# Routed tiles: the gated rows' transpose leads each round, the products come one round later

## The chip, the cores and the metric

The kernel runs on one core of one Trainium2 chip. The metric is the device time of one execution in microseconds, lower is better; of several executions the median counts. Engines are named as in the profile: PE is TensorE (PEld its weight loads), ACT is ScalarE, DVE is VectorE, POOL is GpSimd, SP is the engine that issues most DMAs.

## The reference

Two batches of 1024 tokens of 256 numbers pass through four sublayers: differential attention, a gated feed-forward with a Walsh-Hadamard transform, attention with 16 heads, and a mixture of experts. Each is added to its input and normalized. The change lies in the routed half of the last one:

```python
h12 = jnp.einsum('td,ehd->teh', flat_x, w12)      # 8 experts, 2 x 128 columns each
h1, h2 = jnp.split(h12, 2, axis=-1)
h = jax.nn.silu(h1) * h2
out_e = jnp.einsum('teh,edh->ted', h, w3)
routed_out = jnp.einsum('ted,te->td', out_e, combine).reshape(b, s, d)
```

`combine` is zero but for the two experts that a token has picked.

## The kernel before, in words

The kernel is one program with an instruction stream for each engine, written out by hand; semaphores order the engines against each other, and within an engine the order is that of the code. It does the two batches one after the other.

For the routed half the kernel computes a token only for its two experts. Each pair of a token and an expert gets a row in a list sorted by expert, GpSimd scatters the tokens to it in memory (`xs`), and SP loads the list back into `xg` as 23 tiles (`TILES`) of 128 rows, each tile with one expert (`owner(k)`, read from a register: a register step or two, the REGISTER_ALU rows, and an ISA row that sets the address stand ahead of the product). Then `routed(b)` takes each tile k through these steps:

- TensorE transposes the tile's 256 columns in two pieces (`turn_tokens`, L1033) into PSUM (`xt_bank[k % 2]`).
- The products are made in three passes of a high and a low part (`pass3`, L408 to L410). So ScalarE copies the transposed tile to `xr_h` (L1499), and VectorE subtracts that from it and has `xr_l` (L1916).
- TensorE multiplies with the expert's gate and up weights (`gate_up_tile`: six products, shown as `ps<-E_h,xr_h` and the like, into `xt_bank[2 + k % 2]`).
- ScalarE makes the SiLU (`silu_r`, L1511), VectorE the gated rows `Hr` (L1932).
- TensorE transposes these (`turn_gated`, L1055) into the one bank `ring[0]`. ScalarE copies them to `hr_h` (L1505), VectorE makes `hr_l` (L1925).
- TensorE multiplies with the expert's last weights (`down_tile`: three products, `ps<-E_h,hr_h`, into the one bank `ring[1]`), ScalarE copies the result into `xg` (L1515), and GpSimd stores it to its rows in `ys` (L2347).

The steps of different tiles overlap. Round i of the loop holds, on TensorE, the token transposes of tile i, the gated transpose of tile i - 3, the products of tile i - 1 and the result of tile i - 4. ScalarE's round has xr_h of i, hr_h of i - 3, the SiLU of i - 1 and the result copy of i - 4; VectorE's has xr_l of i, hr_l of i - 3 and Hr of i - 1. Buffers are used in turn by two (`k % 2`). What matters among the waits: the gated transpose waits for the hr_l of the tile before (`rh_lo`), as they share the bank, and for its own Hr (`rm_done`); the product of a tile waits for its xr_l (`rx_lo`); the token transposes wait for the xr_l of two tiles back and for the load of `xg` (`xg_in`); a result's product waits for its hr_l and for the copy of the result before (`ry_copy`).

In the first rounds there is other work too. TensorE makes the last two results of the shared half (`down`) in rounds 0 and 1, VectorE takes these into `X` (`take`, L1632, four instructions, 1.4 us in all), and in rounds 2, 4 and 10 it works out store addresses in three small operations (`destinations`, L1903 to L1908). In the first batch both takes fall into the routed stage, at rounds 1 and 2; in the second batch the stage begins four steps before the end of the shared half, and the second take comes later. What follows the stage on TensorE is the start of the next batch (transposes and projections) in the first batch, and the last four steps of the shared half in the second.

Of the kernel before, what the change touches and what calls it, by code (L numbers as in the profile page):

```python
# [33 lines left out]
P = 128  # L34
# [60 lines left out]
def program(nc, d, ctx):  # L95
# [121 lines left out]
    with ExitStack() as s:  # L217
        Fw_h, Fw_l = [], []
        for i in range(FW_RING):
            Fw_h.append(sb(f"Fw_h{i}", [P, FFN_COLS], F32R, s))  # L220
            Fw_l.append(sb(f"Fw_l{i}", [P, FFN_COLS], F32R, s))
        silu_g = [sb(f"silu_g{i}", [P, HALF], F32, s) for i in range(2)]
        Hf = [sb(f"Hf{i}", [P, HALF], F32, s) for i in range(2)]
        H_h = [sb(f"H_h{i}", [P, HALF], F32R, s) for i in range(H_RING)]
        H_l = [sb(f"H_l{i}", [P, HALF], F32R, s) for i in range(H_RING)]
        E_h = sb("E_h", [P, EXPERTS, FFN_COLS], F32R, s)
        E_l = sb("E_l", [P, EXPERTS, FFN_COLS], F32R, s)
        with ExitStack() as r:
            LG = sb("LG", [P, T], F32, r)
        xr_h = [sb(f"xr_h{i}", [P, KC, P], F32R, s) for i in range(2)]  # L230
        xr_l = [sb(f"xr_l{i}", [P, KC, P], F32R, s) for i in range(2)]
        silu_r = [sb(f"silu_r{i}", [P, P], F32, s) for i in range(2)]
        Hr = [sb(f"Hr{i}", [P, P], F32, s) for i in range(2)]
        hr_h = [sb(f"hr_h{i}", [P, P], F32R, s) for i in range(2)]
        hr_l = [sb(f"hr_l{i}", [P, P], F32R, s) for i in range(2)]
# [538 lines left out]
    def _(pe):  # L774
# [244 lines left out]
        def routed(b):  # L1019
# [16 lines left out]
            def gate_up_tile(k, e):  # L1036
# [6 lines left out]
                for c in range(KC):  # L1043
                    w = tile(c, 2 * P)
                    mm = pass3(pe, xt_bank[2 + k % 2][:, 0:2 * P], xr_h[k % 2][:, c], xr_l[k % 2][:, c],
                               E_h[:, bass.ds(e, 1), w], E_l[:, bass.ds(e, 1), w], c == 0, c == KC - 1)
# [27 lines left out]
            for i in range(TILES + 4):  # L1074
# [4 lines left out]
                if 0 <= i - 3 < TILES:  # L1079
                    turn_gated(i - 3)  # L1080
                if 0 <= i - 1 < TILES:
                    gate_up_tile(i - 1, owner(i - 1))
                if i >= 4:
                    down_tile(i - 4, owner(i - 4))
# [223 lines left out]
    def _(act):  # L1308
# [182 lines left out]
        def routed(b):  # L1491
            N = TILES * b
            for i in range(TILES + 4):
                k = i
                if k < TILES:
                    act.wait_ge(rx_ps, N + k + 1)
                    if k >= 2:
                        act.wait_ge(rg_mm, N + k - 1)
                    nc.scalar.copy(xr_h[k % 2][:], xt_bank[k % 2][:, 0:HID].rearrange("p (c n) -> p c n", c=KC)).then_inc(rx_hi, 1)  # L1499
                k = i - 3  # L1500
# [5 lines left out]
                k = i - 1  # L1506
# [5 lines left out]
                k = i - 4  # L1512
# [109 lines left out]
    def _(dve):  # L1622
# [272 lines left out]
        def routed(b):  # L1895
# [14 lines left out]
            for i in range(TILES + 3):  # L1910
                if i - 2 in [ends[0] for ends in XG_LOADS]:
                    destinations([ends[0] for ends in XG_LOADS].index(i - 2))
                k = i
                if k < TILES:
                    dve.wait_ge(rx_hi, N + k + 1)
                    nc.vector.tensor_tensor(xr_l[k % 2][:], xt_bank[k % 2][:, 0:HID].rearrange("p (c n) -> p c n", c=KC),  # L1916
                                            xr_h[k % 2][:].bitcast(F32), ALU.subtract).then_inc(rx_lo, 1)
# [4 lines left out]
                k = i - 3  # L1922
                if 0 <= k < TILES:
                    dve.wait_ge(rh_hi, N + k + 1)
                    nc.vector.tensor_tensor(hr_l[k % 2][:], ring[0][:, 0:P], hr_h[k % 2][:].bitcast(F32),  # L1925
                                            ALU.subtract).then_inc(rh_lo, 1)
                k = i - 1
# [505 lines left out]
```

## Time and profile before

| | |
|---|---|
| median of 3 runs | 1675.94 us |
| lowest and highest | 1673.62, 1676.69 us |
| the profiled execution | 1674.55 us |
| its span | 1672.70 us |
| mean granted TensorE clock, of full | 0.992 |
| routed stage, first batch (first L1033 to last result copy) | 783.6 to 829.8 |
| routed stage, second batch | 1593.2 to 1638.1 |

The span is what the profile covers of one execution; the rest of the execution's time lies around it. A row of the timeline has the start in us from the span's start, the duration, the engine and line, the operation, output <- input with buffer numbers left out, and how often it is repeated; behind it, in brackets, how long the engine had been idle and what ended that. A matmul's recorded duration is longer than its distance to the next one, since matmuls are pipelined: distances are read from start to start.

### The profile page before, as it was taken

The page shows a single profiled execution, that of the slowest core. Times are in us where ns is not written, and L with a number is a line of the kernel's source. Part 1 is how long each engine was busy: PE and PEld are TensorE (multiplying, and loading weights), DVE is VectorE, ACT ScalarE, POOL GpSimd, SP SyncE. Part 2 cuts the span into 40 slices and gives each one's busy share as a digit, 9 for nine tenths or more (in the row PEclk, how much of TensorE's full clock was granted, in tenths as well). Part 3 has the DMA queues.
Part 4 walks back from the last instruction along what each step waited for, and adds up shares of the span by engine and source line. Part 5 has one row for each costly group of instructions (what it writes and reads, how often), then busy time and mean ns, then how long its engine had stood idle before and what let it go on. Part 6 is the DMA issues. An engine that isn't in the chain of part 4 may idle for free.

```text
span 1672.7 us, 31096 instructions
## 1 busy us (share of the span) xinstructions
PE 1569.3 (94%) x10834; PEld 1354.4 (81%) x10834; DVE 1094.5 (65%) x2693; ACT 933.3 (56%) x2054; POOL 641.3 (38%) x590
## 2 busy tenths in 40 slices
PE   8999999999999899899898999999999989999995
PEld 7888889888887677687777898898988876776784
DVE  7667667676635878473586676666756467875555
ACT  5666565565444577552656656656554346775352
POOL 2646444454460102161535545443555420032531
PEclk9999999999999999999999999999999999999998
DMA  3110000020110423123212000000202113322132
GB/s 130 45 51 17 26 1 16 25 90 1 48 59 15 77 46 71 51 92 121 91 59 92 1 17 26 16 25 1 90 1 67 40 35 63 57 59 100 61 124 98
DMA packets 48195, 88.04 MB, mean 53 GB/s; under 512 B 9600, under 2 KB 30480, under 8 KB 46928
## 3 DMA queue, kind: packets, MB, share of 16 engines
q1 hardware_dynamic: 44320, 76.07, 15.9%
q0 software_dynamic: 3744, 10.26, 1.7%
q8 instruction: 78, 1.28, 0.3%
q14 instruction: 53, 0.43, 0.1%
HBM read 60.18 MB, written 19.76 MB: 48 GB/s over the span
## 4 chain that ended last, share of the span: by engine, by line
PE 67%; DVE 14%; ACT 9%; issue 6%; POOL 2%; ACTq 0%; DMA 0%; DVEq 0%; POOLq 0%; SPq 0%
PE ps L408 16%; PE ps L410 15%; PE ps L409 15%; PE ps L1180 4%; PE ps L1197 4%; PE ps L1140 4%; DVE nmax L1777 3%; ACT E L1394 3%; PE ps L903 2%; ACT PT_h L1376 2%; POOL E L2221 1%; DVE PT_l L1754 1%; DVE On L1697 1%; PE ps L1176 1%; PE ps L829 1%
## 5 line engine op out<-in xcount | busy, mean ns | idle before, releaser
L1394 ACT ACTIVATE E<-ps,nmax 128x128 f32<-128x128 f32 (+7 forms) x256 | 189.1, 742 | 210.5 <-DVE nmax L1777 210.0
L2218 POOL TENSOR_SCALAR E<-E,mixc 128x128 f32<-128x128 f32 (+7 forms) x128 | 97.3, 760 | 402.8 <-DVE mixc L1747 402.8
L1777 DVE TENSOR_REDUCE nmax<-ps 128x1 f32<-128x128 f32 (+7 forms) x256 | 183.2, 749 | 12.5 <-PE ps L878 12.3
L1546 ACT ACTIVATE PT<-ps 128x512 f32<-128x512 f32 x288 | 154.9, 601 | 59.0 <-PE ps L1180 57.5
L2221 POOL TENSOR_TENSOR E<-E 128x128 f32<-128x128 f32 (+7 forms) x128 | 182.6, 1426 | 10.7
L408 PE MATMUL ps<-V_h,PT_h 128*128 128x256 f32 x576 | 167.2, 290 | 0.9 <-DVE O L1759 0.9
L409 PE MATMUL ps<-V_l,PT_h 128*128 128x256 f32 x576 | 163.0, 283 | 0.0
L410 PE MATMUL ps<-V_h,PT_l 128*128 128x256 f32 x576 | 163.0, 283 | 0.0
L408 PE MATMUL ps<-K_h,Q_h 128*128 128x512 f32 (+3 forms) x384 | 147.5, 384 | 8.6 <-ACT E L1394 5.2
L1754 DVE TENSOR_TENSOR PT_l<-ps,PT_h 128x128 fp32r<-128x128 f32 (+7 forms) x128 | 96.7, 756 | 69.5 <-ACT PT_h L1376 68.9
L1981 DVE CUSTOM_DVE_ANT_0 masked<-ps,causal 128x128 bf16<-128x128 f32 (+3 forms) x256 | 111.1, 487 | 42.4 <-PE ps L1140 40.5
L410 PE MATMUL ps<-K_h,Q_l 128*128 128x512 f32 (+3 forms) x384 | 133.3, 347 | 0.0
L409 PE MATMUL ps<-K_l,Q_h 128*128 128x512 f32 (+3 forms) x384 | 132.9, 346 | 0.0
L1140 PE MATMUL ps<-KS,QS 128*128 128x512 f32 (+3 forms) x384 | 111.6, 371 | 7.9 <-issue 5.8
L1180 PE MATMUL ps<-QS,KS 128*128 128x512 f32 (+3 forms) x384 | 112.3, 362 | 0.0
L408 PEld LDWEIGHTS ps<-V_h,PT_h 128*128 128x128 f32 x576 | 109.8, 191 | 2.5 <-issue 1.2
L409 PEld LDWEIGHTS ps<-V_l,PT_h 128*128 128x128 f32 x576 | 109.9, 191 | 0.5
L410 PEld LDWEIGHTS ps<-V_h,PT_l 128*128 128x128 f32 x576 | 109.8, 191 | 0.0
L408 PE MATMUL ps<-XT_h,Fw_h 128*128 128x512 f32 x256 | 103.4, 404 | 5.4 <-DVE XT_l L1628 2.8
L1833 DVE TENSOR_TENSOR Hf<-ps,silu_g 128x512 f32<-128x512 f32 x64 | 44.2, 691 | 93.2 <-PE ps L410 71.7
L903 PE MATMUL ps<-ident,E 128*128 128x128 f32 x576 | 85.0, 274 | 19.0 <-POOL E L2221 18.4
L410 PE MATMUL ps<-XT_h,Fw_l 128*128 128x512 f32 x256 | 102.1, 399 | 0.3 <-issue 0.3
(265 smaller groups left out, 4652.2 us busy)
## 6 DMA issues: line engine op xcount, KB each, us to landing
Wa_raw<-in_wa SPq DMA_DIRECT2D x8, 1024.0 KB, 4.9
Fw_raw<-in_fa SPq DMA_DIRECT2D x32, 256.0 KB, 2.7
E_raw<-in_fe SPq DMA_DIRECT2D x8, 768.0 KB, 7.5
xs<-in_xs SPq DMA_DIRECT2D x2, 2967.0 KB, 12.3
Wo_raw<-in_wo SPq DMA_DIRECT2D x8, 512.0 KB, 3.6
yg<-ys SPq DMA_DIRECT2D x8, 512.0 KB, 5.7
xg<-xs SPq DMA_DIRECT2D x6, 645.0 KB, 8.5
KS<-QK_h SPq DMA_DIRECT2D x56, 64.0 KB
```

The source lines that it names most:

```text
L408: nc.tensor.matmul(out, a_h, b_h, start=start, stop=False, **kw)
L409: nc.tensor.matmul(out, a_h, b_l, start=False, stop=False, **kw)
L410: return nc.tensor.matmul(out, a_l, b_h, start=False, stop=stop, **kw)
L903: mm = nc.tensor.transpose(ps[2][:, tile(kb)], E1[n % 2][:, tile(kb)], ident[:])
L1140: mm = nc.tensor.matmul(bank1(j % RING1)[:, at:at + z - a], QS[:, 2 * (p % Q_PAIRS) + n, tile(i)], KS[:, p % K_PAIRS, a:z], start=at == 0, ...
L1180: mm = nc.tensor.matmul(bank[:, at:at + z - a], KS[:, p % K_PAIRS, tile(kb)], QS[:, 2 * (p % Q_PAIRS) + n, a:z], start=not diagonal and k ...
L1394: nc.scalar.activation(e[:, 0:w], ps[m][:, 0:w], ACT.Exp, bias=nmax[:, s % 4, m:m + 1], accum_out=lsum[:, s % 4, m:m + 1]).then_inc(exp_do ...
L1546: nc.scalar.activation(PT[:, at:at + HALF], bank1(RING1 + n % RING1), ACT.Exp, scale=SCALE1).then_inc(t_used, 1)
L1754: nc.vector.tensor_tensor(PT_l[n % 2][:, 0:w], ps[2][:, 0:w], PT_h[n % 2][:, 0:w].bitcast(F32), ALU.subtract).then_inc(pt_lo, 1)
L1777: nc.vector.tensor_reduce(nmax[:, s % 4, m:m + 1], ps[m][:, 0:(s % NT + 1) * P], AX.X, ALU.max, negate=True).then_inc(nmax_ready[m], 1)
L1981: ins = nc.vector.tensor_tensor_reduce(out=masked[:, j % RING1, cols], in0=scores, in1=causal[:, HALF - (z - a):], scale=-1.0, scalar=3e38 ...
L2221: nc.gpsimd.tensor_tensor(e1, e1, e2, ALU.add).then_inc(p_ready, 1)
```

## The change

The token transposes, xr_h and xr_l of tile i stay in round i. The products of a tile, its SiLU and Hr, its gated transpose, hr_h, hr_l and its result all move to one round later, so the loop has one round more. In each round the gated transpose now leads: on TensorE L1055 stands ahead of the token transposes, on ScalarE hr_h stands ahead of xr_h, on VectorE hr_l ahead of xr_l. `xr_h` and `xr_l` get three buffers, and xr_h waits for the products of three tiles back instead of two. No instruction is added or taken away but for waits.

```diff
@@ -227,8 +227,8 @@
-        xr_h = [sb(f"xr_h{i}", [P, KC, P], F32R, s) for i in range(2)]
-        xr_l = [sb(f"xr_l{i}", [P, KC, P], F32R, s) for i in range(2)]
+        xr_h = [sb(f"xr_h{i}", [P, KC, P], F32R, s) for i in range(3)]
+        xr_l = [sb(f"xr_l{i}", [P, KC, P], F32R, s) for i in range(3)]
...
@@ -1071,17 +1071,17 @@
-            for i in range(TILES + 4):
+            for i in range(TILES + 5):
+                if 0 <= i - 4 < TILES:
+                    turn_gated(i - 4)
                 if i < TILES:
                     turn_tokens(i)
                 if i < 2:
                     down(b, moe_at(b) - 2 + i)
-                if 0 <= i - 3 < TILES:
-                    turn_gated(i - 3)
-                if 0 <= i - 1 < TILES:
-                    gate_up_tile(i - 1, owner(i - 1))
-                if i >= 4:
-                    down_tile(i - 4, owner(i - 4))
+                if 0 <= i - 2 < TILES:
+                    gate_up_tile(i - 2, owner(i - 2))
+                if i >= 5:
+                    down_tile(i - 5, owner(i - 5))
...
@@ -1490,26 +1490,26 @@
+            for i in range(TILES + 5):
+                k = i - 4
                 if 0 <= k < TILES:
                     act.wait_ge(rh_ps, N + k + 1)
                     if k >= 2:
                         act.wait_ge(rd_mm, N + k - 1)
                     nc.scalar.copy(hr_h[k % 2][:], ring[0][:, 0:P]).then_inc(rh_hi, 1)
-                k = i - 1
+                k = i
+                if k < TILES:
+                    act.wait_ge(rx_ps, N + k + 1)
+                    if k >= 3:
+                        act.wait_ge(rg_mm, N + k - 2)
+                    nc.scalar.copy(xr_h[k % 3][:], xt_bank[k % 2][:, 0:HID].rearrange("p (c n) -> p c n", c=KC)).then_inc(rx_hi, 1)
+                k = i - 2
...
@@ -1907,24 +1907,24 @@
-            for i in range(TILES + 3):
+            for i in range(TILES + 4):
                 if i - 2 in [ends[0] for ends in XG_LOADS]:
                     destinations([ends[0] for ends in XG_LOADS].index(i - 2))
+                k = i - 4
+                if 0 <= k < TILES:
+                    dve.wait_ge(rh_hi, N + k + 1)
+                    nc.vector.tensor_tensor(hr_l[k % 2][:], ring[0][:, 0:P], hr_h[k % 2][:].bitcast(F32),
+                                            ALU.subtract).then_inc(rh_lo, 1)
                 k = i
...
```

What moves on TensorE, in a round in the middle of the stage (Hr is the gated rows' transpose, xg the tokens'; REGISTER_ALU and ISA are the register steps ahead of the first product):

```order
 L409 MATMUL ps<-E_l,hr_h 128x256
 L410 MATMUL ps<-E_h,hr_l 128x256
+L1055 MATMUL ps<-ident,Hr 128x128
 L1033 MATMUL ps<-ident,xg 128x128 x2
-L1055 MATMUL ps<-ident,Hr 128x128
 L408 REGISTER_ALU x2
 L408 ISA
```

The gated transpose has passed the two token transposes; the register steps of the first product are right behind these now, and were right behind the gated transpose. In the code after, the gated transpose still carries the waits rh_lo and rm_done, and the pair xg_in and rx_lo.

ScalarE, a round and a half in the middle of the stage, before:

```order
L1499 CAST xr_h0<-ps2 128x256 [waits rg_mm,rx_ps]
L1505 CAST hr_h1<-ps0 128x128 [waits rd_mm,rh_ps]
L1511 ACTIVATE silu_r1<-ps3 128x128 [waits rm_done,rg_mm]
L1515 COPY xg<-ps0 128x256 [waits rd_mm]
L1499 CAST xr_h1<-ps2 128x256 [waits rg_mm,rx_ps]
L1505 CAST hr_h0<-ps0 128x128 [waits rd_mm,rh_ps]
```

and after (the line numbers have moved: L1499 is hr_h now, L1505 xr_h):

```order
L1515 COPY xg<-ps0 128x256 [waits rd_mm]
L1499 CAST hr_h1<-ps0 128x128 [waits rd_mm,rh_ps]
L1505 CAST xr_h0<-ps2 128x256 [waits rg_mm,rx_ps]
L1511 ACTIVATE silu_r1<-ps3 128x128 [waits rm_done,rg_mm]
L1515 COPY xg<-ps0 128x256 [waits rd_mm]
L1499 CAST hr_h0<-ps0 128x128 [waits rd_mm,rh_ps]
```

hr_h follows the result copy directly; xr_h stood between them. VectorE at the start of the stage in the first batch (X is the take, dest the store addresses):

```order
-L1916 TENSOR_TENSOR xr_l<-ps,xr_h 128x256 x2
+L1921 TENSOR_TENSOR xr_l<-ps,xr_h 128x256 x2
 L1632 TENSOR_TENSOR X<-ps,X 128x256 x4
-L1932 TENSOR_TENSOR Hr<-ps,silu_r 128x128
 L1903 SCALAR_TENSOR_TENSOR dest<-expert_f,xg 128x2
 L1906 TENSOR_TENSOR dest<-dest,xg 128x2
 L1908 CAST dest_i<-dest 128x2
-L1916 TENSOR_TENSOR xr_l<-ps,xr_h 128x256
+L1921 TENSOR_TENSOR xr_l<-ps,xr_h 128x256
 L1632 TENSOR_TENSOR X<-ps,X 128x256 x4
 L1932 TENSOR_TENSOR Hr<-ps,silu_r 128x128
```

The Hr of tile 0 stood ahead of the address operations, and now stands behind them, behind xr_l of tile 2 and behind the second take.

## Rows read from the trace of the kernel before

**Rows 1.** The page: the span, and the busy time of TensorE.
```profile
span 1672.7 us, 31096 instructions
...
PE 1569.3 (94%) x10834; PEld 1354.4 (81%) x10834; DVE 1094.5 (65%) x2693; ACT 933.3 (56%) x2054; POOL 641.3 (38%) x590
```

**Rows 2.** Timeline of TensorE, second batch: the transposes of a fast round.
```profile
1610.34 0.38 PE L1033 MATMUL ps<-ident,xg 128*128 128x128 f32 x2
1610.56 0.27 PE L1055 MATMUL ps<-ident,Hr 128*128 128x128 f32 x1
...
1611.74 0.38 PE L1033 MATMUL ps<-ident,xg 128*128 128x128 f32 x2
```

**Rows 3.** The same view: first product of tiles 4 and 22 in both batches.
```profile
793.28 0.36 PE L408 MATMUL ps<-E_h,xr_h 128*128 x1
...
824.17 0.38 PE L408 MATMUL ps<-E_h,xr_h 128*128 x1
...
1602.61 0.38 PE L408 MATMUL ps<-E_h,xr_h 128*128 x1
...
1632.08 0.38 PE L408 MATMUL ps<-E_h,xr_h 128*128 x1
```

**Rows 4.** Timeline of all engines, second batch: two rounds, the steps of the loop.
```profile
1623.81 0.37 ACT L1515 COPY xg<-ps 128x256 f32<-128x256 f32 x1
...
1624.08 0.38 ACT L1499 CAST xr_h<-ps 128x256 fp32r<-128x256 f32 x1
...
1624.34 0.28 ACT L1505 CAST hr_h<-ps 128x128 fp32r<-128x128 f32 x1
...
1624.49 0.42 DVE L1916 TENSOR_TENSOR xr_l<-ps,xr_h 128x256 fp32r<-128x256 f32 x1 [0.44 <-issue]
...
1624.83 0.28 DVE L1925 TENSOR_TENSOR hr_l<-ps,hr_h 128x128 fp32r<-128x128 f32 x1
...
1625.59 0.38 PE L408 MATMUL ps<-E_h,xr_h 128*128 x1
...
1626.96 0.37 ACT L1515 COPY xg<-ps 128x256 f32<-128x256 f32 x1
```

**Rows 5.** Timeline, first batch: TensorE stands idle until hr_l is done.
```profile
821.93 0.28 DVE L1925 TENSOR_TENSOR hr_l<-ps,hr_h 128x128 fp32r<-128x128 f32 x1
...
822.36 0.30 PE L1055 MATMUL ps<-ident,Hr 128*128 128x128 f32 x1 [0.29 <-DVE hr_l L1925]
...
822.78 0.38 PE L408 MATMUL ps<-E_h,xr_h 128*128 x1
```

**Rows 6.** Timeline, second batch: the drain, without xr_h and xr_l.
```profile
1634.80 0.37 ACT L1515 COPY xg<-ps 128x256 f32<-128x256 f32 x1 [0.75 <-PE ps L410]
1635.07 0.27 ACT L1505 CAST hr_h<-ps 128x128 fp32r<-128x128 f32 x1
1635.37 0.29 DVE L1925 TENSOR_TENSOR hr_l<-ps,hr_h 128x128 fp32r<-128x128 f32 x1 [1.00 <-ACT hr_h L1505]
1635.41 0.38 PE L408 MATMUL ps<-E_h,hr_h 128*128 x1 [0.54 <-ACT xg L1515]
```

**Rows 7.** Timeline, second batch: eight small products; xr_l and products of tile 2.
```profile
1560.00 0.35 PE L1015 MATMUL ps<-both,tri 128*128 128x64 bf16 x8
...
1598.66 0.42 DVE L1916 TENSOR_TENSOR xr_l<-ps,xr_h 128x256 fp32r<-128x256 f32 x1
...
1599.41 0.38 PE L408 MATMUL ps<-E_h,xr_h 128*128 x1 [0.74 <-DVE xr_l L1916]
```

**Rows 8.** Timeline of VectorE: Hr of tile 0, second batch; second take, first batch.
```profile
789.11 1.41 DVE L1632 TENSOR_TENSOR X<-ps,X 128x256 f32<-128x256 f32 x4
...
1598.01 0.28 DVE L1932 TENSOR_TENSOR Hr<-ps,silu_r 128x128 f32<-128x128 f32 x1
```

**Rows 9.** Timeline of ScalarE, first batch: one of four late xr_h.
```profile
814.19 0.37 ACT L1499 CAST xr_h<-ps 128x256 fp32r<-128x256 f32 x1 [0.32 <-PE ps L1033]
```

**Rows 10.** Windows: time, busy us of each engine (instructions), granted clock, DMA share, GB/s.
```profile
1630.00:1640.00 10.00, 8.12 (x42) 6.51 (x41) 2.37 (x8) 3.86 (x14) 6.52 (x7) 0.83 0.22 80
```

More of the change, by code:

```diff
@@ L1044, in gate_up_tile @@
                     w = tile(c, 2 * P)
-                    mm = pass3(pe, xt_bank[2 + k % 2][:, 0:2 * P], xr_h[k % 2][:, c], xr_l[k % 2][:, c],
+                    mm = pass3(pe, xt_bank[2 + k % 2][:, 0:2 * P], xr_h[k % 3][:, c], xr_l[k % 3][:, c],
                                E_h[:, bass.ds(e, 1), w], E_l[:, bass.ds(e, 1), w], c == 0, c == KC - 1)
@@ L1492, in routed @@
             N = TILES * b
[L1493 to L1500, printed above, removed]
+            for i in range(TILES + 5):
+                k = i - 4
                 if 0 <= k < TILES:
@@ L1511, in routed @@
                     nc.scalar.activation(silu_r[k % 2][:], xt_bank[2 + k % 2][:, 0:P], ACT.Silu).then_inc(rs_done, 1)
-                k = i - 4
+                k = i - 5
                 if 0 <= k < TILES:
@@ L1915, in routed @@
                     dve.wait_ge(rx_hi, N + k + 1)
-                    nc.vector.tensor_tensor(xr_l[k % 2][:], xt_bank[k % 2][:, 0:HID].rearrange("p (c n) -> p c n", c=KC),
-                                            xr_h[k % 2][:].bitcast(F32), ALU.subtract).then_inc(rx_lo, 1)
+                    nc.vector.tensor_tensor(xr_l[k % 3][:], xt_bank[k % 2][:, 0:HID].rearrange("p (c n) -> p c n", c=KC),
+                                            xr_h[k % 3][:].bitcast(F32), ALU.subtract).then_inc(rx_lo, 1)
                 if i == 1:
@@ L1921, in routed @@
                     take(b, 1)
[L1922 to L1927, printed above, removed]
+                k = i - 2
                 if 0 <= k < TILES:
```

## The prediction, made before the changed kernel ran

> **What bounds the kernel now.** I read the page first [rows 1]: TensorE is busy 94% of a span of 1672.7 us, so work taken off other engines is worth nothing unless TensorE waits for it. The change touches only the routed stage, one for each of the two batches, so I read that stage next, in time order. At its fast rounds TensorE needs 1.40 us for a tile (two L1033 transposes, one L1055 transpose, six first products and three second ones): from one L1033 pair to the next, 1610.34 to 1611.74 [rows 2]. The average round is longer. With G the start of a tile's first product, and G counted from tile 4 to tile 22 (18 rounds), the first batch takes 824.17 - 793.28 = 30.89 us, or 1.716 a round, and the second 1632.08 - 1602.61 = 29.47 us, or 1.637 [rows 3]. So 0.24 to 0.32 us of each round is not work of TensorE.
>
> What closes the rounds is a loop over four engines [rows 4]. ScalarE copies the result of one tile (L1515, 1623.81), then takes xr_h (L1499, 0.27 later), then hr_h (L1505, 0.26 later). VectorE does xr_l first (1624.49) and hr_l behind it (1624.83, 0.49 after hr_h's start, ending 1625.11). The L1055 transpose of the next gated tile needs that hr_l, since one bank holds it. Then come G (1625.59) and the next copy (1626.96, 1.37 after G). That is 3.15 us, and two rounds pass in it. The step from hr_l's end to G is 0.48 there and usually 0.57: with TensorE idle, hr_l ends at 822.21, L1055 starts at 822.36 and G is at 822.78 [rows 5]. The 0.48 belongs to one tile in six, whose expert number needs one register step less. With 0.57 the loop is 0.27 + 0.26 + 0.49 + 0.28 + 0.57 + 1.37 = 3.24, a round of 1.62, near the 1.637 measured. So the loop bounds the stage, not TensorE's work.
>
> **The change, part by part.** No arithmetic is added or removed; instructions move, and xr gets a third buffer.
>
> ScalarE: hr_h now stands ahead of xr_h, right behind the copy. L1515 to hr_h is then 0.27, as in the drain, where no xr_h stands between (1634.80 to 1635.07) [rows 6]. This takes 0.26 out of the loop. VectorE: hr_l stands ahead of xr_l. From hr_h's start to hr_l's it is 0.30 when nothing stands between (1635.07 to 1635.37) [rows 6], against 0.49. This takes out 0.19. Together 0.45 us in two rounds.
>
> xr_h and xr_l now come last, but the products that read them come one round later. They start some 0.3 later in a round and have a round of 1.4 more: no cost. The third buffer is what makes that free of a wait for the products of two tiles back.
>
> TensorE: L1055 leads and the L1033 pair follows. Before, the pair was issued ahead of the wait for hr_l and ran while TensorE waited. Now it is issued behind that wait, with two waits of its own (xg_in, rx_lo), and G follows it. I call the added time e. It isn't in the trace, so I bound it. Lower end 0: from L1055's start to G there are 0.42 us [rows 5], and L1055 with the pair needs 0.33 of the array (the pair 0.22, 1610.34 to 1610.56, so 0.11 each) [rows 2]. Below zero makes no sense, since nothing is taken out there. Upper end 0.35: G is 0.33 behind its release when the release comes at the product's own wait (xr_l ends 1599.08, G 1599.41) [rows 7], and 0.57 when it comes at L1055's, so L1055 with its waits is worth 0.24; a pair would be that and one transpose of 0.11 more. In between: a result product is 0.24 behind its last wait (copy ends 1635.17, product 1635.41) [rows 6], where the 0.33 above has one wait more still to pass, so a wait is some 0.09; eight small products with their weight loads start within 0.35 - 0.17 us, 0.025 apart [rows 7]. One or two waits and two issues give 0.14 to 0.23. I take 0.18.
>
> The Trainium skill, "TensorE: Matmul & The Clock Gate", section "Wait — 56ns, not 53.3ns?", says that small products never start closer than about 25 ns, and that with hardware decode off a product costs its sequencer about 62 ns. The row above agrees with the first; by the second, two transposes would put 0.12 instead of 0.05 into e, and a round would be 0.04 longer.
>
> The new loop is 0.27 + 0.30 + 0.28 + 0.57 + 0.18 + 1.37 = 2.97, a round of 1.49. With e = 0 it is 2.79, below 1.40 a round, so TensorE's work would bound; with e = 0.35 it is 3.14, or 1.57. In the last two of the 18 rounds no L1033 is left: 1.40 each. So tiles 4 to 22 take 16 x 1.49 + 2 x 1.40 = 26.6 us. Against rows 3 that is 2.8 less in the second batch and 4.3 less in the first.
>
> The opening. Before, Hr of tile 0 starts at 1598.01 [rows 8], with three index operations between it and xr_l of tile 2 (1598.66) [rows 7]. Now these and xr_l come first, some 0.8 us, so it ends at about 1599.1; in the first batch the second take of the shared rows (1.41 us at 789.11) [rows 8] comes ahead of it too, and it ends at about 790.1. L1055 leads TensorE's round and holds G of tile 2 until 0.15 + 0.42 behind that, with some of e: 0.4 and 1.3 later than now. Before, the next rounds had waits of their own (G of tile 4 in the second batch, 1602.61, is 3.2 behind that of tile 2, 1599.41), and these now overlap: by my chain of steps G of tile 4 comes 0.2 earlier in the second batch and 0.2 later in the first. Net 0; bounds 0.4 less and 2 more for both. The extra round costs nothing else: only L1033 runs further ahead; products, L1055 and results keep their distance, and the drain is the same, bound by the copy and the one result bank (1634.80 to 1635.41) [rows 6].
>
> First batch: there xr_h starts 0.3 late in every fourth round though its transpose was long done (814.19) [rows 9]. That is why its rounds are 0.08 longer, 1.4 in 18. Behind hr_h such a gap would hide; on hr_h it would not. I keep half, 0.7.
>
> What follows the stage is TensorE's in both batches (the next projections, the last four chunks), so nothing covers the gain or takes it up. Sum: -2.8 - 4.3 + 0.7 = **-6.4 us**. The profiled execution took 1674.55, its span and 1.85 around it, so it would take 1668.2; it lay 1.39 under the median of the runs. From the median of 1675.94 I forecast **1669.5 us**.
>
> **The rivals.**
> (a) TensorE's work bounds the stage: e near 0. It needs L1055's wait not to hold up what stands behind it. For it: room in the array. Against it: in 822.36 to 822.78 G is 0.42 behind L1055 though its operands had been ready, so the stall does delay what follows [rows 5]. Rounds of 1.40 give 25.2 in each batch, 4.3 + 5.7 less: 1666.0. 15%. The Trainium skill, "Perfetto Trace Analysis", section "Tensor Engine Instruction (MATMUL, LD_WEIGHTS)", has matmuls wait in a queue with the sequencer free to go on, which would mean this case; the same page notes extra wait instructions where several engines are waited for, and the 0.42 speaks for those.
> (b) The gain is eaten: e = 0.35 (16 x 1.57 + 2.8 = 27.9, so 1.5 + 3.0 less), the opening costs 1, all of 1.4 stays in the first batch, and TensorE's clock falls once more. In 1630 to 1640, with the sparse drain, the granted clock was 0.83 of the 2.4 GHz level, so part of that stretch ran at 1.2 GHz [rows 10]: 10 x 0.17 = 1.7 us of time at most; I take 1. The new opening in the first batch leaves TensorE with little work for 3 us, much as the drain does. The sum is -4.5 + 1.4 + 1 + 1 = -1.1: 1674.8. 20%. The skill's "TensorE" page, section "Part 4: PE-mode transpose", says that transposes do not count as busy for the clock as products do, which would add to this risk; no run here shows it yet.
> (c) Slower. The removed 0.45 is outweighed from e = 0.45 on. If each of the pair's waits and each transpose costs as much as L1055 with its waits (0.24), e is 0.72 or more: (0.72 - 0.45) / 2 = 0.135 over 32 rounds is 4.3 more; less 0.9 for the four rounds without L1033: 1679.3. Against it: the small products 0.025 apart. 8%.
> (d) The loop isn't what closes the rounds and nothing moves: 1676. Against it: 1.62 by the loop, 1.637 measured. 4%.
>
> **How the numbers follow.** My case, with e from 0.1 to 0.25, has 53% and lies from 1667.5 to 1672; the likeliest single value is 1669.5. The range runs from (a), a little under it, to behind (b): 1665.5 to 1675.5. A measurement of this kernel can tell about 0.2% (3.4 us) from no change: faster is my case and (a), 0.68; the same is most of (b) and (d), 0.24; slower is (c), 0.08.
>
> **What would show it.** In the profile after: G of tiles 4 to 22 some 1.49 apart, both batches nearly alike; L1515 to hr_h 0.27; hr_h to hr_l 0.30; hr_l's end to G 0.75. Rounds of 1.40 mean (a), a last step near 1.0 or more (b) or (c). G of tile 2 should come later than now, G of tile 4 about where it is. I would be wrong if hr_h waited for L1055 rather than for the copy ahead of it, or if the clock fell inside the stage.

## The result, and the profile after

The changed kernel is slower on this chip. Its median is 1681.85 us (1681.17 to 1685.34, 5 runs) against 1675.94 us for the kernel before on the same chip, a ratio of 1.0042 with a 95% interval of 1.0031 to 1.0053. The forecast was 1669.5, with a range up to 1675.5. The profiled execution of after took 1681.17 us.

The page of after gives the same work in a longer span. The columns are as in [rows 1], which had 1672.7 and 1569.3:

```profile
span 1679.4 us, 31094 instructions
...
PE 1573.6 (94%) x10834; PEld 1358.7 (81%) x10834; DVE 1095.5 (65%) x2693; ACT 931.6 (55%) x2054; POOL 642.0 (38%) x590
```

The first product of tiles 4 and 22 in both batches, the rows that answer to [rows 3]:

```profile
792.92 0.36 PE L408 MATMUL ps<-E_h,xr_h 128*128 x1
...
826.03 0.38 PE L408 MATMUL ps<-E_h,xr_h 128*128 x1
...
1605.64 0.36 PE L408 MATMUL ps<-E_h,xr_h 128*128 x1
...
1637.61 0.38 PE L408 MATMUL ps<-E_h,xr_h 128*128 x1
```

The 18 rounds take 33.11 and 31.97 us, where before took 30.89 and 29.47 and the forecast was 26.6. So of the 6.6 us between the two profiled executions 4.7 lie here. (Aligned instruction by instruction on ScalarE, after loses 3.3 us between 720 and 840 and 3.6 between 1560 and 1640; the rest of the span nets to less than 1 us.) Short rounds are as short as forecast: of the 18 in the first batch eleven are 1.40 to 1.54, two 1.59 and 1.80. But five, mostly every third, are 2.62 to 2.88 us. The timeline of one of them (TensorE's and ScalarE's rows that matter, with weight loads left out; L1505 is xr_h in this kernel, L1499 hr_h):

```profile
804.69 0.38 PE L1033 MATMUL ps<-ident,xg 128*128 128x128 f32 x2
...
804.83 0.38 PE L408 MATMUL ps<-E_h,xr_h 128*128 x1
...
805.84 0.37 ACT L1505 CAST xr_h<-ps 128x256 fp32r<-128x256 f32 x1 [0.51 <-PE ps L1033]
...
806.95 0.28 PE L410 MATMUL ps<-E_h,xr_l 128*128 x1
807.38 0.28 ACT L1511 ACTIVATE silu_r<-ps 128x128 f32<-128x128 f32 x1 [1.17 <-PE ps L410]
807.55 0.37 ACT L1515 COPY xg<-ps 128x256 f32<-128x256 f32 x1
...
808.17 0.38 PE L408 MATMUL ps<-E_h,hr_h 128*128 x1 [0.94 <-ACT xg L1515]
```

The token transposes start at 804.69, and ScalarE takes them 1.15 later; in the rounds of this stage where nothing is late it is 0.42 to 0.52, in ten of 18 it is 1.07 to 1.87. The products that begin at 804.83 are seen by the SiLU at 807.38, 2.55 later instead of 1.01. ScalarE stood idle for 1.17 of that, and TensorE had gone on to the products of the next tile (last start 806.95), until it had nothing left that was released and waited 0.94 for the copy. The times of the semaphore updates in the trace say the same: the pair's update comes at 805.82, and five more, from five different groups of matmuls, all come between 807.36 and 807.56, once TensorE stands still. TensorE's starts kept their distance of 0.12 us; the word of its work came late, and in a burst. (The end of a matmul in the trace is modelled, so the trace can't tell whether only the updates were late or the results too.) The waits of the first batch's stage, 783 to 832 (engine and line, what it waited for, us in total, times, longest):

```profile
ACT silu_r L1511 <- PE ps L410: 11.3, 17, 1.2
...
ACT xr_h L1505 <- PE ps L1033: 7.4, 9, 2.2
...
PE ps L408 <- ACT xg L1515: 6.1, 8, 0.9
```

The last line, the result product behind the copy, is the row that TensorE pays; before, it was 1.7 in 3 waits. The late xr_h of [rows 9] was a mild form of this: in the first batch's stage nine updates of TensorE are late in before, by 0.49 us at most, and 31 in after.

### The profile page after: what moved, and what is told of

It is laid out like the page before. It is cut to its first block, busy times and chain, and to the rows that moved or that the text cites. A ratio compares the mean times of both kernels' runs of the same rounds, so it can differ in the third digit from the quotient of the medians.

```text
span 1679.4 us, 31094 instructions
## 1 busy us (share of the span) xinstructions
PE 1573.6 (94%) x10834; PEld 1358.7 (81%) x10834; DVE 1095.5 (65%) x2693; ACT 931.6 (55%) x2054; POOL 642.0 (38%) x590
## 4 chain that ended last, share of the span: by engine, by line
PE 67%; DVE 14%; ACT 9%; issue 6%; POOL 2%; ACTq 0%; DMA 0%; DVEq 0%; POOLq 0%; SPq 0%
PE ps L408 16%; PE ps L410 15%; PE ps L409 15%; PE ps L1180 4%; PE ps L1197 4%; PE ps L1140 4%; DVE nmax L1777 3%; ACT E L1394 3%; PE ps L903 2%; ACT PT_h L1376 2%; POOL E L2221 1%; DVE PT_l L1754 1%; PE ps L1176 1%; DVE On L1697 1%; PE ps L829 1%
## 5 line engine op out<-in xcount | busy, mean ns | idle before, releaser
L410 PE MATMUL ps<-V_h,PT_l 128*128 128x256 f32 x576 | 162.7, 283 | 0.0
L410 PE MATMUL ps<-K_h,Q_l 128*128 128x512 f32 (+3 forms) x384 | 133.4, 347 | 0.0
L410 PEld LDWEIGHTS ps<-V_h,PT_l 128*128 128x128 f32 x576 | 109.6, 190 | 0.0
L410 PE MATMUL ps<-XT_h,Fw_l 128*128 128x512 f32 x256 | 102.6, 401 | 0.1
```

The lines of the kernel that those rows point to most:

```text
L410: return nc.tensor.matmul(out, a_l, b_h, start=False, stop=stop, **kw)
```

## The experiments

Eighteen runs on five further chips, which I name by number; the first measurement was on one more. "G4 to 22" is the time of the 18 rounds in the first and the second batch, each from the one execution that was profiled. Each "Measured" begins with the ratio of the run's median to that of the kernel before on the same chip, with its 95% interval.

### Which part of the change does the harm (chip 15)

depth_only takes from the change only this, with the old order in each round:

```diff
-                if 0 <= i - 1 < TILES:
-                    gate_up_tile(i - 1, owner(i - 1))
+                if 0 <= i - 2 < TILES:
+                    gate_up_tile(i - 2, owner(i - 2))
```

(and the same shift of all that follows the products, and three buffers).

> Products one round later and three buffers for xr, but the old order inside a round (TensorE: token transposes, then the gated one; ScalarE: xr_h, then hr_h; VectorE: xr_l, then hr_l). Theory 1 (TensorE's increments of semaphores come late once its products run on without a break, so the change loses because it closed the breaks): the old loop of 3.24 us in two rounds stands, TensorE still breaks off in most rounds, so 1674 to 1677, like before. Rival A (the pair of token transposes behind the gated transpose's wait does the harm): like before or a little faster, 1672 to 1676. Rival B (the later products and the deeper overlap do the harm): like the changed kernel, about 1682.

Measured: 1.0003 (0.9994 to 1.0011), G4 to 22 29.25 and 29.18, a round of 1.62. Depth alone does nothing, and the round is the 1.62 that the prediction's loop of before gives.

pe_order_old is the whole change but for TensorE's order:

```diff
-                if 0 <= i - 4 < TILES:
-                    turn_gated(i - 4)
                 if i < TILES:
                     turn_tokens(i)
                 if i < 2:
                     down(b, moe_at(b) - 2 + i)
+                if 0 <= i - 4 < TILES:
+                    turn_gated(i - 4)
```

> The whole change but TensorE's order, which is the old one: token transposes ahead of the gated transpose. The loop by its steps is 0.27 + 0.30 + 0.28 + 0.57 + 1.37 = 2.79 in two rounds, so TensorE has no break left. Theory 1: as slow as the changed kernel or slower, 1681 to 1685, with rounds of 1.42 in a row and then one of over 2.5. Rival A: the harm is gone, rounds of 1.40 to 1.45, 1666 to 1670. Rival B: about 1682.

Measured: 0.9960 (0.9948 to 0.9972), 26.04 and 26.12, no long round.

act_dve_order_old is the whole change with xr_h ahead of hr_h and xr_l ahead of hr_l, as before.

> The whole change but ScalarE's and VectorE's order, which is the old one: xr_h ahead of hr_h, xr_l ahead of hr_l. TensorE has the new order. The loop is 3.24 + 0.15 (the pair of transposes behind the wait, as measured: hr_l's end to the product 0.72 instead of 0.57) = 3.39, 1.70 a round, with a break of TensorE in every round. Theory 1: no long rounds; 1.70 a round against 1.64 and 1.72 before: 1675 to 1679, faster than the changed kernel. Rival A: as slow as the changed kernel or slower, 1682 to 1685. Rival B: 1682 or more.

Measured: 1.0026 (1.0016 to 1.0035), 31.06 and 31.13, even rounds of 1.73. TensorE's new order without ScalarE's and VectorE's costs 0.11 a round over depth_only; that is the price of the pair behind hr_l's wait (0.22 in the two rounds of the loop, where I had put 0.18), with nothing to pay it back.

order_only has the new order on all three engines, with the old distance of the products and two buffers.

> The new order inside a round on all three engines, but the products stay where they were (one round after the tile's transposes) and xr has two buffers. The loop through hr is 2.97 in two rounds as in the changed kernel; xr_l of a tile is done some 0.3 later and its product waits for it in the next round. Theory 1: TensorE has few breaks, so late increments and long rounds as in the changed kernel: 1679 to 1684. Rival A: about 1682 too. Rival B: the harm goes, 1670 to 1675.

Measured: 0.9965 (0.9953 to 0.9978), 27.03 and 26.98, a round of 1.50, no long round. So the new order was fast with the old depth, and the new depth was fast in pe_order_old, which packs the stage even more closely (1.45 a round). No part of the change explained the long rounds, and theory 1, which had pe_order_old at 1681 to 1685, did not hold on this chip. I had not yet asked whether the chip did.

### The changed kernel again, with other variants (chips 10 and 6)

> The changed kernel once more, unaltered, on another chip than the first measurement had. In the first measurement every third round of the routed stage was 2.6 to 3.0 us long, since ScalarE saw TensorE's finished transposes and products up to 1.5 us late. Theory A, the lateness belongs to this program (to its order on the three engines together with its depth): G of tiles 4 to 22 takes 31 to 33 us again in both batches, and the ratio to the kernel before is 1.003 to 1.006. Theory B, it belongs to the chip on which the first measurement was made: no long rounds here, 26 to 27 us for the 18 rounds, ratio about 0.996, as the two variants pe_order_old and order_only had on their chip.

> The kernel before once more, unaltered, for a profile on the same chip as after_again. By theory A (a matter of the program) the rounds of tiles 4 to 22 take 30.9 and 29.5 us as in its first profile, xr_h late in every fourth round of the first batch among them. By theory B (a matter of the first chip) the late xr_h are gone and both batches take 29.2 to 29.5 us, as depth_only did.

> The kernel before with only ScalarE's hr_h ahead of xr_h and VectorE's hr_l ahead of xr_l; TensorE's order, depth and buffers as before. If the gain of pe_order_old and order_only is the 0.45 us that this takes out of the loop of the result copy, then by 0.27 + 0.30 + 0.28 + 0.57 + 1.37 = 2.79 the loop falls below TensorE's own 1.40 a round, and if nothing else binds the rounds are 1.40 to 1.45: 25.2 to 26.1 us for tiles 4 to 22, ratio 0.995 to 0.997. The rival: with the products only one round behind the token transposes, xr_l now comes too late for the products that follow the gated transpose (it ends some 0.3 later in the round), and TensorE waits there: rounds of 1.55 or more, 28 us, ratio 0.998 to 1.000; that would be the reason for the products one round later.

after_held adds one wait to the token transposes:

```diff
+                if k >= 3:
+                    pe.wait_ge(rs_done, N + k - 2)
                 pe.wait_ge(xg_in[load], 16 * (len(XG_LOADS[load]) - 1) * (b + 1))
```

> The changed kernel with one wait more on TensorE: the token transposes of tile k wait for the SiLU of tile k - 3, which keeps TensorE from running ahead of ScalarE by more than that. If the signals come late because TensorE's queue of ready work never empties (it stood 0.14 us between pair and products in the rounds ahead of a long one, against 0.20 to 0.37 in others), the long rounds go and each round costs one wait of about 0.09 more: 1.5 to 1.6 a round, 27 to 28.5 us for tiles 4 to 22, ratio 0.998 to 1.000. If the lateness comes from something else in the order of the changed kernel, the long rounds stay: 31 to 34 us, ratio 1.003 or more. If the long rounds are absent in after_again too, this only prices the wait.

Measured on chip 10: after_again 1.0016 (1.0007 to 1.0024), 31.49 and 29.78, with long rounds (its profiled execution, 1681.93, was the longest of twelve with a median of 1676.91); before_again, one execution, 30.12 and 30.20, late xr_h again; sv_order_only 1.0006 (0.9996 to 1.0017), 31.18 and 31.29, not the 25.2 to 28 expected. after_held 1.0036 (1.0024 to 1.0049), 31.78 and 31.75, in even rounds of 1.7 to 2.0: in 46 tiles no late signal (no update of TensorE over 0.15 us late; the SiLU follows its products by 1.01 throughout), but the wait cost 0.3 a round, not 0.09. Its rows show why (line numbers are two higher here):

```profile
811.85 0.28 ACT L1513 ACTIVATE silu_r<-ps 128x128 f32<-128x128 f32 x1 [0.64 <-PE ps L410]
...
812.22 0.41 PE L1035 MATMUL ps<-ident,xg 128*128 128x128 f32 x2
...
812.64 0.38 PE L408 MATMUL ps<-E_h,xr_h 128*128 x1
...
813.65 0.28 ACT L1513 ACTIVATE silu_r<-ps 128x128 f32<-128x128 f32 x1 [0.61 <-PE ps L410]
```

SiLU to transposes 0.37, to the products 0.42, to the next SiLU 1.01: 1.80, a loop of one round that I had closed myself. I had costed the wait and not the loop.

These runs did not decide it. By the words of after_again's expectation, long rounds on a second chip spoke for the program (theory A); theory B, that they belong to the first chip alone, was wrong. But sv_order_only missed its gain too, with nothing changed on TensorE, and the variants that had been fast were not among them. So these were run beside the changed kernel, on chip 6:

> The changed kernel, unaltered, beside the two variants that were fast, on one and the same chip. Theory B (late signals belong to the chip, for any program that packs TensorE densely): if this is a chip with late signals, all three have long rounds and lie at 1.000 to 1.005 of the kernel before; if it is one without, all three are at 0.995 to 0.997, this one with rounds of 1.45 to 1.50 and 26 to 27 us for tiles 4 to 22. Theory A (they belong to this program's order with its depth): this one has long rounds and 30 us or more, the other two none, whatever the chip.

> The whole change but for TensorE's order (token pair ahead of the gated transpose), as in pe_order_old, now on the same chip as after_c. Theory A: 26 us for tiles 4 to 22, ratio 0.996, no long rounds. Theory B on a chip with late signals: products and transposes seen up to 1.5 us late here too, 29 us or more, ratio 1.000 or above; on a chip without them 26 us and 0.996.

> The new order on all three engines, products not later, two buffers, as in order_only, now on the same chip as after_c. Theory A: 27 us for tiles 4 to 22, ratio 0.9965, no long rounds. Theory B on a chip with late signals: 29 us or more, ratio 1.000 or above; on a chip without them 27 us and 0.9965.

> Only ScalarE's and VectorE's order new, as in sv_order_only, which took 31.2 us for tiles 4 to 22 with late signals. On a chip with late signals that again, 1.000 to 1.003. On a chip without them (theory B) rounds of 1.40 to 1.55, 25.5 to 28 us, ratio 0.995 to 0.998.

Measured: after_c 1.0045 (1.0033 to 1.0057), pe_order_old_c 1.0022 (1.0011 to 1.0033), order_only_c 1.0024 (1.0009 to 1.0040), sv_order_only_c 1.0019 (1.0005 to 1.0032). The two programs that gained 0.4% on chip 15 lose 0.2% on chip 6, with G4 to 22 at 32.27 and 32.14, and 32.06 and 29.92. (after_c has 32.73 and 30.72, sv_order_only_c 32.05 and 29.79.) That settles it between this program's order and the chip: the lateness is a property of where a kernel runs, and hits each of the four orders that pack the stage.

### What in TensorE's work brings it on (chip 13)

> The changed kernel, unaltered, as the witness on the chip of the next three. With late signals (as on three chips of four so far): long rounds of 2.5 to 3.0 us, 30 to 33 us for tiles 4 to 22, ratio 1.002 to 1.005. On a chip without them: rounds of 1.40 to 1.50, 26 to 27 us, ratio 0.995 to 0.997; that would be the first time that the changed kernel itself is seen there.

const_expert:

```diff
-                return (packs_e[k // PACK] >> (3 * (k % PACK))) & (EXPERTS - 1)
+                return k % EXPERTS
```

> The changed kernel with the expert of each tile a constant (k modulo 8) instead of a register: this leaves out the choice of the expert in the routed products, and with it seven register and address instructions of TensorE in each round, with no change in the array's work. Theory R (the late signals come from the register instructions, or from the number of instructions that TensorE's sequencer handles): no long rounds though the stage is as dense or denser, 1.30 to 1.45 a round, 23.5 to 26 us for tiles 4 to 22 on a chip where after_d has long rounds. Theory D (they come when the array's work runs without a break, whatever the instructions): still long rounds, 29 us or more. Either way the time outside the two stages is as in after_d.

wide_products:

```diff
-                for c in range(KC):
-                    w = tile(c, 2 * P)
-                    mm = pass3(pe, xt_bank[2 + k % 2][:, 0:2 * P], xr_h[k % 3][:, c], xr_l[k % 3][:, c],
-                               E_h[:, bass.ds(e, 1), w], E_l[:, bass.ds(e, 1), w], c == 0, c == KC - 1)
+                w = slice(0, 4 * P)
+                mm = pass3(pe, xt_bank[2 + k % 2][:, 0:4 * P], xr_h[k % 3][:, 0], xr_l[k % 3][:, 0],
+                           E_h[:, bass.ds(e, 1), w], E_l[:, bass.ds(e, 1), w], True, True)
```

> The changed kernel with the six gate and up products of 256 columns made as three of 512: as many columns, half as many product instructions and address steps. It leaves out the second half of each tile's contraction in these products. Theory R (number of instructions): few or no long rounds, 1.40 to 1.50 a round, 25 to 27 us for tiles 4 to 22. Theory D (array without a break): long rounds as in after_d, 30 us or more.

two_pass leaves the L410 products out of the routed tiles.

> The changed kernel without the third pass of each routed product (the low part of xr and hr times the high part of the weights), which leaves out three of nine products, 0.36 us of array work a round. The next copy then comes some 0.36 earlier, so the loop is 2.97 - 0.36 = 2.61, or 1.31 a round, against 1.04 of array work: TensorE has a break in every round. Both theories R and D expect no long rounds: 23.5 to 25 us for tiles 4 to 22. If long rounds come here too, neither holds, and the lateness is a matter of the chip's signals at any density of this stage.

This chip has no late signals, so the question they were made for (is it the number of instructions or the array without a break) stays unanswered. Their times still count. after_d, the unaltered change, is at **0.9966** (0.9954 to 0.9977), 1662.69 against 1667.92, with G4 to 22 at 26.50 and 26.72. const_expert: 0.9929 (0.9909 to 0.9949), 25.04 and 24.95, nearly every round 1.40 or 1.41, so without the register steps TensorE's work bounds the stage (they stand in the loop's step from hr_l to G, which falls to 0.59 here). wide_products: 0.9954 (0.9940 to 0.9968), 26.38 and 26.19: half as many product instructions of as many columns change nothing much. two_pass: 0.9928 (0.9907 to 0.9949), 25.32 and 25.21, or 1.41 a round and not the 1.31 that the loop less 0.36 gives; what holds it there I did not follow up.

The loop of the change as it runs where signals are in time (timeline of after_d, second batch):

```profile
1600.74 0.37 ACT L1515 COPY xg<-ps 128x256 f32<-128x256 f32 x1
...
1601.01 0.27 ACT L1499 CAST hr_h<-ps 128x128 fp32r<-128x128 f32 x1
...
1601.31 0.29 DVE L1916 TENSOR_TENSOR hr_l<-ps,hr_h 128x128 fp32r<-128x128 f32 x1 [0.34 <-ACT hr_h L1499]
...
1602.10 0.27 PE L1055 MATMUL ps<-ident,Hr 128*128 128x128 f32 x1
...
1602.21 0.38 PE L1033 MATMUL ps<-ident,xg 128*128 128x128 f32 x2
...
1602.34 0.37 PE L408 MATMUL ps<-E_h,xr_h 128*128 x1
...
1603.70 0.37 ACT L1515 COPY xg<-ps 128x256 f32<-128x256 f32 x1
```

0.27, 0.30, 0.29, 0.74 and 1.36: 2.96, against 2.97 in the prediction. TensorE shows no idle time in these rows: what was released earlier keeps it busy until L1055. The step from hr_l's end to G is 0.69 to 0.73 in most rounds, and 0.57 in the last two of the first batch, where no token transposes stand behind the wait.

### What the late signals need (chip 7)

The traces held the next idea. From the semaphore update times I took each update of TensorE against the recorded end of its matmul, over whole executions, about 2000 updates in each of the 20 traces. On the four chips with late signals every update more than 0.15 us late lies in one of four stretches or within 4 us behind it: the two in which GpSimd issues the 16 indirect stores of the tokens to `xs` (L2338, about 739 to 760 in the first batch), and the two with the 23 indirect stores of the results to `ys` (L2347, about 794 to 834). (In stores_last, below, they lie where the stores of `ys` have moved.) None lies elsewhere, though TensorE is dense elsewhere too; and the eight traces of chips 13 and 15 have none at all, with the same stores. (Where a record is missing this counts an update too many, in the four stretches as well; the none outside them stands.) And aligned instruction by instruction, order_only_c loses on order_only 3.9 us between 720 and 760, 8.1 between 760 and 840, 4.8 between 1560 and 1640, and below 0.1 us in nearly every other 40 us of the span. So the last two runs move the indirect stores. plain_stores:

```diff
-                nc.gpsimd.indirect_dma_start(d["ys"], bass.IndirectOffsetOnAxis(dest_i[:, k:k + 1], 0), xg[:, k, 0:HID],
-                                             None).then_inc(yr_out, 16)
...
+            for k in range(TILES):
+                sp.wait_ge(ry_copy, TILES * b + k + 1)
+                sp.dma_start(d["ys"][k * P:(k + 1) * P], xg[:, k, 0:HID]).then_inc(yr_out, 16)
```

> The changed kernel with the 23 indirect stores of the routed results (GpSimd, L2347) replaced by 23 plain stores of the same rows, issued by SP to consecutive rows: this leaves out the placing of the results, so the output is wrong in the routed part. The 16 indirect stores of the tokens to xs (L2338), ahead of the stage, stay; they show what chip this is. In the traces so far every late signal of TensorE lies in one of the four stretches in which GpSimd issues indirect DMAs (739 to 760 and 794 to 834 us, and the same in the second batch), and none elsewhere. Theory I (the lateness needs GpSimd's indirect DMAs at the same time): on a chip with late signals the first stretch (739 to 760) shows them, but the routed stage has none: rounds of 1.40 to 1.55, 26 to 27 us for tiles 4 to 22. Theory D (unbroken TensorE work alone): long rounds as before, 30 us or more. On a chip without late signals in the first stretch the run tells nothing of it.

stores_last:

```diff
-                pool.wait_ge(ry_copy, TILES * b + k + 1)
+                pool.wait_ge(ry_copy, TILES * b + TILES)
```

> The changed kernel with the first indirect store of the routed results held until the last result of the batch is copied; nothing is left out. The 23 stores of 1.27 us then run in the 29 us behind the stage, which makes the end later by about 25 us in the second batch (ratio about 1.015). Theory I: on a chip with late signals the routed stage has none (26 to 27 us for tiles 4 to 22), and in the first batch they appear behind it, in the 29 us of the stores, if TensorE works without a break there. Theory D: they stay in the routed stage (30 us or more). On a chip without them in 739 to 760 the run tells nothing of it.

Measured: plain_stores 0.9966 (0.9952 to 0.9981), 26.50 and 26.76. stores_last 1.0208 (1.0191 to 1.0225), 26.58 and 26.76; that is 35 us more than before and not the 25 expected, since the first batch loses time behind its stage as well. The changed kernel itself did not run on chip 7. Is it a chip of the kind with late signals? Before took 1675.09 there, as on the other chips with late signals, and the windows say so too. Columns: time, busy us of PE, PEld, DVE, ACT and POOL with instruction counts, granted clock, DMA share, GB/s. First after (first chip), with the stretch ahead of the stage, then the stage:

```profile
750.00:760.00 10.00, 8.10 (x44) 6.75 (x43) 2.64 (x4) 2.05 (x3) 7.87 (x8) 0.95 0.29 102
800.00:810.00 10.00, 8.32 (x64) 7.38 (x63) 5.17 (x17) 5.55 (x21) 4.86 (x6) 1.00 0.18 66
```

after_d (chip 13, none late):

```profile
750.00:760.00 10.00, 10.00 (x61) 8.84 (x60) 4.70 (x7) 3.51 (x7) 7.87 (x8) 1.00 0.31 107
800.00:810.00 10.00, 10.00 (x84) 9.72 (x84) 6.92 (x21) 7.36 (x28) 6.37 (x8) 1.00 0.26 93
```

plain_stores (chip 7), the stage without indirect stores:

```profile
750.00:760.00 10.00, 8.39 (x46) 6.79 (x45) 3.03 (x4) 2.20 (x4) 7.62 (x7) 1.00 0.26 93
800.00:810.00 10.00, 10.00 (x84) 9.66 (x83) 6.53 (x21) 7.53 (x28) 0.00 (x0) 1.00 0.27 94
```

stores_last (chip 7), the stage, and the stretch behind it to which the indirect stores have moved:

```profile
800.00:810.00 10.00, 10.00 (x83) 9.55 (x81) 6.93 (x22) 7.34 (x28) 0.00 (x0) 1.00 0.01 2
...
840.00:850.00 10.00, 5.15 (x13) 3.44 (x12) 1.50 (x2) 1.37 (x2) 7.62 (x8) 0.69 0.30 107
```

In 750 to 760 chip 7 behaves as the first chip does: TensorE starts 46 matmuls where chip 13 starts 61. One stage later, without indirect stores, it starts the same 84 as chip 13. The bytes moved are the same, 94 GB/s against 93, so the traffic by itself is not it. And where the indirect stores are moved, the trouble appears anew: 13 matmuls in 840 to 850 (in part that is the clock, granted 0.69 here: it falls only once TensorE has stood idle). Timeline there, the next batch's projections:

```profile
839.84 0.40 PE L410 MATMUL ps<-XT_h,Wa_l 128*128 128x512 f32 x1
...
841.99 0.69 ACT L1340 ACTIVATE Q_h<-ps,ba 128x512 fp32r<-128x512 f32 x1 [4.27 <-remote]
842.71 0.75 DVE L1677 SCALAR_TENSOR_TENSOR Q_l<-ps,ba,Q_h 128x512 fp32r<-128x512 f32 x1 [4.21 <-issue]
...
843.52 0.56 PE L408 MATMUL ps<-XT_h,Wa_h 128*128 128x512 f32 x1 [3.28 <-DVE Q_l L1677]
```

TensorE's last product of a run starts at 839.84, ScalarE takes a result only at 841.99 after 4.27 us idle, and TensorE stands 3.28. In plain_stores, on the same chip, the same projections run without a break, 46 matmuls in 828 to 838, and ScalarE waits 0.68 to 0.69 between its results. The lateness goes and comes with GpSimd's indirect stores, on a chip that has it: that is shown, with one gap: that the changed kernel would have had it in its stage on chip 7 is inferred from before's time and from 750 to 760. Not separated: whether it is GpSimd's making of the stores, its queue, or rows scattered in memory, since SP's plain stores differ in all three.

The Trainium skill, "SBUF — State Buffer", section "SBUF: two separate sides", says of the compute engines that "PE, ACT, and DVE's dedicated pair never wait on anyone". That is about ports to memory; the rows here (TensorE idle 3.28, ScalarE 4.27) show engines held up all the same while GpSimd issues stores, as far as the trace tells by signals that come late.

## Why the prediction was wrong, step by step

| kernel | chip | ratio | G4 to 22, us |
|---|---|---|---|
| before / after | first | 1.0042 | 30.89, 29.47 / 33.11, 31.97 |
| after_again | 10 | 1.0016 | 31.49, 29.78 |
| after_c | 6 | 1.0045 | 32.73, 30.72 |
| after_d | 13 | 0.9966 | 26.50, 26.72 |
| forecast | | 0.9962 | 26.6, 26.6 |

The ratios are of medians, the times of rounds of one execution each.

**What held.** ScalarE's step (0.27), VectorE's (0.30), TensorE's with the pair behind the wait (0.57 + e, where I took e as 0.18; measured 0.69 to 0.73 in most rounds of after_d and 0.74 in the one shown, so e is 0.12 to 0.17), and the round: 26.50 and 26.72 against 26.6 on chip 13. The drain is the same (4.54 from G of tile 22 to the last result product in after_d, 4.60 in before), and the opening nets to about nothing: from the first product to G of tile 4 there are 6.40 and 5.80 in after against 6.40 and 6.14. Rival (a), e of nothing, is not what the change does; pe_order_old, which has no such e, came near its 25.2 (26.1), and const_expert reached it (25.0). Rival (c), a loop longer than before, did not come about: e is far from 0.45. It named the right sign and nearly the right time (1679.3) for a wrong reason, which is luck.

**The step that failed** is the one on the late xr_h of [rows 9]: "Behind hr_h such a gap would hide; on hr_h it would not. I keep half, 0.7." It took four late starts in one batch for small, local gaps that a reordering could hide. They were signals of TensorE that arrive late, and the term was mis-sized: 33.11 and 31.97 against 26.6 are 6.5 and 5.4 us, **11.9 in place of 0.7**. With the 7.1 that the two batches were to gain, that turns the stage's gain into a loss of 4.7. The row itself held the warning: the transposes were "long done" and ScalarE idle, waiting for TensorE, so something else than the transposes was late, and I gave it no rival of its own and no price beyond what the old order had shown.

Why it grows so is in part argued, in part shown. In before, 0.24 to 0.32 us of an average round was not TensorE's work; after_c ran some 34 matmuls on end ahead of its first late update; after_held, which stops TensorE in every round, had none in the same stage with the same stores on a chip that has them. The late updates in the two stages, counted in each trace, go the same way: 12 in before and 11 in before_again, 36 and 30 in the two runs of sv_order_only, 40 in order_only_c, 59, 55 and 56 in after and its repeats, 61 in pe_order_old_c. So the fewer breaks TensorE's stream has there, the more signals are late, and the change takes breaks out. That the breaks of before are what kept its lateness small is the reading that fits, not a thing measured apart (after_held also spreads the work and the stores over a longer time): before's rounds on these chips are still 0.02 to 0.10 above 1.62.

**The gain where nothing is late** is 5.2 us (1667.92 to 1662.69), not 6.4. Before itself has no trace on such a chip, but depth_only, whose loop is that of before, takes 29.25 and 29.18 there, and from these to 26.50 and 26.72 it is 5.2 as well. So 1.6 and 0.3 of the gains that I read off [rows 3] were lateness that this kind of chip has not, and I had taken off only 0.7 for it.

**Clock.** In after it did not fall inside the stage (granted 1.00 in each 10 us from 780 to 830). At the stage's opening in the second batch it did in after_d, and not in order_only: granted 0.58 against 1.00 in 1584 to 1588, and from the first transposes to the first product 5.0 us instead of 3.4. TensorE had waited about as long for the load of `xg` just before, 2.32 us and 2.25. The prediction had one more fall down as a risk under (b), but for the new opening in the first batch, where none came; what decides this one I have not found.

**A version better than both:** none for all chips. Of those that leave nothing out, pe_order_old has the lowest ratio where signals are in time (0.9960, not told apart by its interval from order_only's 0.9965 or the change's 0.9966), and it loses 0.22% on chip 6. On the chips with late signals none was faster than before.

## What to carry to other kernels

A wait on an engine whose work is "long done" is not a small gap but a different fault; give it a rival of its own, look where else in the trace it occurs and what runs at those times, before costing a change that makes the stage denser. Measure a change of half a per cent on more than one chip, with its variants beside it on each: here one program gained 0.4% on one and lost 0.2% on another. And ask of each term of a sum whether its size holds only for the order in which it was seen. And where a stage issues indirect stores from GpSimd, a stream on TensorE without breaks may be worth less than its rounds say.

## What was unexpected of the hardware

Chips fall into two kinds for this kernel. Before took 1667.92 and 1668.28 us on chips 13 and 15, and 1673.57, 1674.41, 1675.09 and 1675.94 on 10, 6, 7 and the first, though order_only and order_only_c agree within 0.1 us over hundreds of microseconds outside the stretches with indirect stores. The change gains on chip 13 and loses on the first, 10 and 6. Whether it is the chip itself or something that comes with it, such as where memory lies, these runs can't tell.

In the token stores' stretch TensorE itself slows on the chips with late signals: matmuls start 0.7 us apart with nothing to wait for, where 0.12 is usual (timeline of TensorE, plain_stores, 756 to 758):

```profile
755.99 0.28 PE L410 MATMUL ps<-Fw_h,H_l 128*128 128x256 f32 x1
756.11 0.28 PE L408 MATMUL ps<-Fw_h,H_h 128*128 128x256 f32 x1
756.84 0.36 PE L409 MATMUL ps<-Fw_l,H_h 128*128 128x256 f32 x1 [0.46 <-issue]
757.55 0.37 PE L410 MATMUL ps<-Fw_h,H_l 128*128 128x256 f32 x1 [0.35 <-issue]
```

Aligned with order_only on chip 15, before loses 4.4 us there in the first batch, before_again 2.2 and after 4.0. It lies outside the change. It may well be where the next gain in this kernel is, for the chips of this kind.
